# Row-tiled scores in two softmax attentions: queries and keys of four heads stacked together, max and exp passes interleaved, masks grouped, loops unrolled

## Chip, cores and metric

The kernel runs on one NeuronCore of one Trainium2 chip. The metric is the device time of one execution in microseconds, and lower is better. The kernel before was timed three times.

## What is computed

The reference is a two-layer decoder on x of 4 sequences x 256 tokens x 128 channels. Each layer is attention, cross attention and a mixture of experts. The change touches two of the six parts: the first (called at0 in the kernel: rotary self attention) and the fifth (xa1: causal cross attention). Both have 16 heads of 8 channels and a plain softmax over 256 keys:

```python
x = x + _L0_attn_ref(_layernorm(x), wq, wk, wv)             # at0, touched
x = x + _L0_xattn_ref(_layernorm(x), ctx, ctx, ...)         # xa0
x = x + _L0_ffn_ref(_layernorm(x), ...)                     # ff0
x = x + _L1_attn_ref(_layernorm(x), ...)                    # at1
x = x + _L1_xattn_ref(_layernorm(x), ctx, mask, ...)        # xa1, touched
x = x + _L1_ffn_ref(_layernorm(x), ...)                     # ff1
# at0
scores = jnp.einsum('bqhd,bkhd->bhqk', q, k) / jnp.sqrt(HEAD_DIM)
out = jnp.einsum('bhqk,bkhd->bqhd', softmax(scores), xv)
# xa1: the same with a causal mask, then a projection
m = mask[:, None, :, None] + future[None, None, :, :]
scores = jnp.where(m != 0, NEG, scores)
ctx = jnp.einsum('bhqk,bkhd->bqhd', softmax(scores), v).reshape(b, s, d)
return ctx @ WO
```

## The kernel before

One program per engine, tied by semaphores. The kernel goes through the six parts in order. An attention works on one sequence (b, "batch", 256 tokens) at a time, and in it on head after head; `step(k, b, follow)` is one slot of a software pipeline of 32 slots per batch, of which each batch overlaps the second 16 with the first 16 of the next. So 80 slots run per attention, 16 of them filling and 16 of them emptying. What one head passes through:

- **Stacking.** TensorE copies the 8 query rows of four heads (a "group" g; head h = 4g + j) to rows 32j to 32j+23 in PSUM with a selection matrix `selr`, in float32r with a high and a low part (`stack`, L1135 to L1140: one matmul of the high part, one of the low part). Three copies (high, low and high parts for the one operand, the matching ones for the other) keep the accuracy of float32 in one pass. ScalarE moves the result to `qs` (`stacked_queries`, L529) and to `ks` (`stacked_keys`, L483).
- **Key copies.** The score matmul contracts over all 128 rows, so for each head the keys must be zero outside its 32 rows. SyncE copies the 32 rows of head h from `ks` to `km[:, h, :]`, a buffer of zeros, with one DMA per head (`attention_keys`, L286 to L304): 64 DMAs per attention.
- **Max pass** (slot k = h, L1171 to L1190): scores with queries on the partitions, two matmuls of 256 columns (one for each 128 queries) into PSUM bank h % 2; in xa1 each is followed by a bfloat16 matmul that adds the causal mask (L1189). VectorE takes the negative maximum of each query (L788, one instruction per head) into `nmax`.
- **Merge** (slots 5, 9, 13, 17): TensorE transposes the maxima of a group (L1198), and VectorE adds them to `qs` as a 25th row (L795), where `ks` holds ones (bias `one_row`).
- **Exp pass** (slot k = h + 7, L1201 to L1213): scores with keys on the partitions, two matmuls of 256 columns into bank 2 + h % 2, in xa1 again each with a mask matmul (L1212). ScalarE applies exp (L546) into `prob`.
- **Values** (slots 12 + 4g and 13 + 4g, L1227): float32 matmuls with 32 output columns per head, four heads beside each other on the four column tiles of the array, first the keys 0 to 127, in the next slot the keys 128 to 255.
- **Outputs** (slots 27, 28): transposes back to tokens (L1249), division and residual on VectorE (L802 to L819); in xa1 also slots 30, 31 with the projection (L1254, L1259, L823).

Every engine runs its instructions in order. The score banks are two per pass, so the matmuls of head h wait for the reduction (or exp) of head h - 2. `pipelined` (L227) lays the slots out: batch 0 and batch 3 are written out, batches 1 and 2 are a hardware loop (`Fori`). The fill of batch 0 has the stacking of its keys already behind it (`stack_first_keys`) and stacks the first queries ahead of slot 0. In a batch, slots 3, 4, 9, 10 stack queries and slots 7, 8, 15 stack keys of the next one.

## Time and profile before

| what | us |
|---|---|
| three timed executions, median | 581.61 |
| lowest, highest | 576.68, 583.44 |
| profiled execution, span | 581.3 |
| PE busy in it | 504.7 (87%) |
| DVE busy | 442.6 (76%) |
| ACT busy | 250.3 (43%) |
| POOL busy | 121.2 (21%) |

The profiled execution is described by its span of 581.3 us, 0.3 under the median of the timed ones. PE is TensorE's matmuls, PEld its weight loads (they overlap PE), DVE VectorE, ACT ScalarE, POOL GpSimd, SP the DMA queue of SyncE. A matmul is listed with its pipeline latency, so the distance between the starts of two neighbours, not the time listed, is what one costs in a stream. Matmuls of float32r are listed as f32. In this profile at0 spans about 31 to 117 us, xa1 about 238 to 355 us.

### The profile page before, as it was taken

How to read it: one execution, taken by the hardware profiler on the slowest of the kernel's cores; microseconds unless marked ns; L12 is line 12 of the kernel's file. 1: busy time of each engine (PE TensorE's matmuls, PEld its weight loads, DVE VectorE, ACT ScalarE, POOL GpSimd, SP SyncE). 2: the span in 40 equal slices, each digit the busy share in tenths (PEclk: the TensorE clock that was granted, in tenths of full speed). 3: DMA queues.
4: the chain of work that ended last, by engine and by line, in shares of the span. 5: the costliest groups of instructions: out<-in, count | busy, mean ns of one | idle time of the engine just before them, and what ended most of it. 6: DMA issues, size and time to landing. Idle time of an engine off the chain costs nothing.

```text
span 581.3 us, 9298 instructions
## 1 busy us (share of the span) xinstructions
PE 504.7 (87%) x2860; PEld 366.1 (63%) x2860; DVE 442.6 (76%) x939; ACT 250.3 (43%) x488; POOL 121.2 (21%) x147
## 2 busy tenths in 40 slices
PE   2889999789926865799999987999999999999995
PEld 1566776567404542577777765777767676767673
DVE  4396777574696876575656648899999999999996
ACT  1556675422542110334444444464544545362651
POOL 5060001111555251200000000021212111212112
PEclk9989999978976776799999997999999999999998
DMA  8711110003000000101000000000000000000001
GB/s 295 299 38 33 28 27 19 1 1 145 1 1 0 1 1 0 25 21 27 22 18 19 19 1 1 1 1 2 0 0 0 0 0 0 0 0 2 0 1 36
DMA packets 12750, 15.77 MB, mean 27 GB/s; under 512 B 4136, under 2 KB 11432, under 8 KB 12080
## 3 DMA queue, kind: packets, MB, share of 16 engines
q1 hardware_dynamic: 12288, 14.53, 8.0%
q10 hardware_dynamic: 432, 0.85, 0.4%
q8 instruction: 17, 0.28, 0.2%
q14 instruction: 13, 0.11, 0.1%
HBM read 10.65 MB, written 0.52 MB: 19 GB/s over the span
## 4 chain that ended last, share of the span: by engine, by line
PE 53%; DVE 22%; issue 15%; ACT 5%; POOL 2%; DMA 1%; DVEq 1%; ACTq 0%; POOLq 0%
PE ps L1185 7%; PE ps L1227 6%; PE ps L1208 5%; DVE bigr L1034 4%; PE ps L1444 3%; PE ps L1445 2%; PE ps L1446 2%; PE ps L1189 2%; POOL xnT L449 2%; DVE big L1043 2%; PE ps L1383 2%; PE ps L1344 2%; PE ps L1249 1%; PE ps L1212 1%; PE ps L1463 1%
## 5 line engine op out<-in xcount | busy, mean ns | idle before, releaser
L788 DVE TENSOR_REDUCE nmax<-ps 128x2 f32<-128x512 f32 x128 | 86.5, 690 | 47.8 <-PE ps L1189 31.1
L1036 DVE TENSOR_TENSOR bigr<-big,bigr 128x512 fp32r<-128x512 f32 x128 | 111.1, 868 | 4.4
L546 ACT ACTIVATE big<-ps 128x512 f32<-128x512 f32 (+1 forms) x128 | 68.9, 545 | 76.2 <-PE ps L1212 51.1
L657 ACT ACTIVATE big<-ps,b 128x512 f32<-128x512 f32 x128 | 85.3, 694 | 19.3 <-DVE bigr L1036 11.1
L449 POOL TENSOR_TENSOR xnT<-xnT,big 128x512 f32<-128x512 f32 x32 | 44.1, 1377 | 174.5 <-DVE big L1043 174.4
L1185 PE MATMUL ps<-bigr,qs 128*128 128x256 f32 x256 | 69.3, 345 | 4.4 <-DVE nmax L788 2.1
L1208 PE MATMUL ps<-qs,bigr 128*128 128x256 f32 x256 | 65.6, 328 | 1.1 <-ACT big L546 1.1
L1185 PEld LDWEIGHTS ps<-bigr,qs 128*128 128x128 f32 x256 | 45.2, 196 | 25.4 <-DVE nmax L788 14.5
L1444 PE MATMUL ps<-k1hi,w1hi 128*128 128x512 f32 x128 | 55.7, 435 | 0.4
L1034 DVE CAST bigr<-big 128x512 fp32r<-128x512 f32 x128 | 53.6, 419 | 0.9 <-ACT big L657 0.9
L1445 PE MATMUL ps<-k1hi,w1lo 128*128 128x512 f32 x128 | 51.9, 406 | 0.0
L1446 PE MATMUL ps<-k1lo,w1hi 128*128 128x512 f32 x128 | 51.8, 405 | 0.0
L1461 PE MATMUL ps<-bigr,w2hi 128*128 128x512 f32 x128 | 50.8, 397 | 0.2
L1463 PE MATMUL ps<-bigr,w2hi 128*128 128x512 f32 x128 | 50.5, 395 | 0.0
L1462 PE MATMUL ps<-bigr,w2lo 128*128 128x512 f32 x128 | 50.2, 392 | 0.0
L1208 PEld LDWEIGHTS ps<-qs,bigr 128*128 128x128 f32 x256 | 44.8, 194 | 3.6 <-ACT big L546 2.2
L1227 PE MATMUL ps<-big,vaug 128*32 128x256 f32 (+1 forms) x512 | 37.3, 364 | 1.4 <-ACT big L546 1.4
L347 POOL COPY vaug<-v_tok 128x64 f32 x32 | 7.3, 240 | 135.4 <-PE ps L1227 135.4
L1444 PEld LDWEIGHTS ps<-k1hi,w1hi 128*128 128x128 f32 x128 | 24.9, 195 | 12.9 <-issue 6.1
L650 ACT ACTIVATE big<-ps 128x512 f32<-128x512 f32 x32 | 19.2, 600 | 26.5 <-PE ps L1452 26.4
L1189 PE MATMUL ps<-trib,identb 128*128 128x256 bf16 (+1 forms) x128 | 30.4, 256 | 0.0
L1212 PE MATMUL ps<-trib,identb 128*128 128x128 bf16 x128 | 29.4, 230 | 0.0
(192 smaller groups left out, 886.9 us busy)
## 6 DMA issues: line engine op xcount, KB each, us to landing
bigr<-ks SPq DMA_DIRECT2D x128, 32.0 KB, 1.9
wi<-in_wi SPq DMA_DIRECT2D x1, 2048.0 KB, 7.8
wo<-in_wo SPq DMA_DIRECT2D x1, 2048.0 KB, 12.2
big<-in_sel SPq DMA_DIRECT2D x1, 1024.0 KB, 8.8
wo<-in_w SPq DMA_DIRECT2D x1, 1024.0 KB, 4.8
wi<-in_w SPq DMA_DIRECT2D x1, 1024.0 KB, 8.2
x<-in_x SPq DMA_DIRECT2D x1, 512.0 KB, 5.0
ctxT<-in_ctxT ACTq DMA_DIRECT2D x1, 512.0 KB, 6.6
```

The lines of the kernel that those rows point to most:

```text
L546: act.activation(prob[:, h % 8, c], ps[:, 2 + h % 2, c], ACT.Exp, scale=DH ** -0.5).then_inc(s(L + "_exp"), 1)
L657: act.activation(gel[:, c, :], ps[:, c, :], ACT.Gelu_apprx_tanh, bias=b1[:, u % E1, c:c + 1]).then_inc(s("ff1_gel"), 1)
L788: v.tensor_reduce(nmax[:, :, g, col:col + 1], ps[:, k % 2, :].rearrange("p (t k) -> p t k", t=TPB), AX.X, ALU.max, negate=True).then_inc(s ...
L1034: v.tensor_copy(ghi[:, u % 2, c, :], gel[:, c, :]).then_inc(s("ff1_ghi"), 1)
L1036: v.tensor_tensor(glo[:, u % 2, c, :], gel[:, c, :], ghi[:, u % 2, c, :].bitcast(f32), ALU.subtract).then_inc(s("ff1_glo"), 1)
L1185: last = pe.matmul(ps[:, h % 2, at:at + T], qs[:, h // HPG, t * P:t * P + P], km[:, h, :], start=True, stop=not causal)
L1208: last = pe.matmul(ps[:, 2 + h % 2, at:at + T], km[:, h, t * P:t * P + P], qs[:, h // HPG, :], start=True, stop=not causal)
L1227: last = pe.matmul(ps[QUAD * j:QUAD * j + QUAD, 4, (g % 2) * T + first:(g % 2) * T + T], vaug[:, t, h, :], prob[:, h % 8, place(t) * T + f ...
L1444: pe.matmul(ps[:, k, :], w1hi[:, e, f], xhi[:, c], start=True, stop=False)
L1445: pe.matmul(ps[:, k, :], w1lo[:, e, f], xhi[:, c], start=False, stop=False)
L1446: pe.matmul(ps[:, k, :], w1hi[:, e, f], xlo[:, c], start=False, stop=True).then_inc(s("ff1_up"), 1)
L1463: last = pe.matmul(o, w2hi[:, e, k, :], glo[:, u % 2, k, :], start=False, stop=(k == FC - 1))
```

## The change

Queries and keys of a group are stacked into one buffer `qk` [128, group, side, 256] by four matmuls that contract over the 32 rows of the group's channels only, in one PSUM bank; one ScalarE instruction moves both. A score matmul of head h takes the 32 rows 32j to 32j+31 of `qk` for both operands, so the zero-filled `km`, its fill and its 128 DMAs are gone. In each slot the two max matmuls of head k and the two exp matmuls of head k - 7, which lie on neighbouring 32-row tiles of the array, alternate. In xa1 the mask matmuls of both passes follow the four score matmuls, and the second exp matmul has only the 128 query columns that the mask leaves. The value matmuls of a group stand together in one slot (k % 4 = 0). All four stacks of batch 0 come ahead of slot 0; later stacks come in slots 13, 15, 3 and 9. The 80 slots are written out, with no loop.

```diff
+FIRST_BANKS = (6, 7, 4, 5)
...
-        qs = sb("qs", [P, G, T], f32r)
-        ks = sb("ks", [P, G, T], f32r)
-        km = bigr[:, 4096:8192].rearrange("p (h t) -> p h t", h=H)
+        qk = sb("qk", [P, G, 2, T], f32r)
...
+        AFT_SLOT = 2
+        STACK_SLOTS = {13: (1, 0), 15: (1, 1), 3: (0, 2), 9: (0, 3)}
+        STACKED_SLOTS = {14: (1, 0), 0: (0, 1), 4: (0, 2), 10: (0, 3)}
...
+        def pipelined(slot, beside={}):
+
+            for b in range(B + 1):
                 for k in range(H):
-                    if not first:
-                        step(H + k, b - 1, follow)
-                    step(k, b, follow)
-
-            for k in range(H // 2 - 1, H):
-                step(k, -1, True)
-            if before_first:
-                before_first()
-            batch(0, True, True)
-            if before_loop:
-                before_loop()
-            with engine.Fori(1, B - 1) as b:
-                batch(b, False, True)
-            batch(B - 1, False, False)
-            for k in range(H, 2 * H):
-                step(k, B - 1, None)
-                if k in beside:
-                    beside[k]()
+                    slot(k, b)
+                    if b == B and k in beside:
+                        beside[k]()
...
-            def attention_keys(L):
-
-                def keys(b, g):
-                    if g % 2 == 0:
-
-                        sp.wait_ge(s(L + "_ksev"), 1 + 2 * b + g // 2 + 1)
-                        sp.sem_inc(s("keys_stacked"), 1)
-
-                    sp.wait_ge(s(L + "_s"), H * b + HPG * g + HPG)
-                    for j in range(HPG):
-                        rows = slice(QUAD * j, QUAD * j + QUAD)
-                        sp.dma_start(km[rows, HPG * g + j, :].bitcast(f32), ks[rows, g, :].bitcast(f32)
-                                     ).then_inc(s(L + "_km%d" % g), 16)
-
-                for g in range(G):
...
-            pool.memset(km[:, :, :].bitcast(f32), 0.0).then_inc(s("const"), 1)
...
+            def evacuate_stack(L, b, g, bank=6):
+
+                act.wait_ge(s(L + "_stk"), G * b + g + 1)
+                act.activation(qk[:, g, :, :], ps[:, bank, :].rearrange("p (a t) -> p a t", a=2),
+                               ACT.Identity, bias=one_row[:, :]).then_inc(s(L + "_stkev"), 1)
...
+                    if stack := stacked(STACKED_SLOTS, k, b):
+                        evacuate_stack(L, *stack)
+                    if b == B and not causal and k == AFT_SLOT + 1:
                         evacuate_aft_sums(0)
-                    if 7 <= k < H + 7:
-                        h = k - 7
-                        if there(b):
-                            act.wait_ge(s(L + "_s"), H + H * b + h + 1)
-
-                            if h % HPG == 0:
-                                act.wait_ge(s(L + "_pv"), G + G * b + h // HPG - 1)
-
-                            c = slice(P if causal else 0, TPB * T)
-                            act.activation(prob[:, h % 8, c], ps[:, 2 + h % 2, c], ACT.Exp, scale=DH ** -0.5
-                                           ).then_inc(s(L + "_exp"), 1)
-
-                    if k in (5, 7) and there(b):
-                        stacked_queries(b, 2 + k // 7)
-                    if k in (12, 15) and follow:
-                        stacked_queries(b + 1, k // 15)
-                    if k in (8, 15) and follow and there(b):
-                        stacked_keys(L, b + 1, int(k == 15))
-                    if k in (17, 25) and there(b):
-
-                        gg = k // 8 - 2
-                        act.wait_ge(s(L + "_pv"), G + G * b + 2 * gg + 2)
+                    if head := lagging(k, b, 7):
...
+                def stack(b, g, bank=6):
+
+                    if g == 0 and b * T % HALF == 0:
+                        pe.wait_ge(*half_ready[b * T // HALF])
+                    if b > 0:
+                        pe.wait_ge(s(L + "_stkev"), G * b + g)
+                    rows, c = slice(QUAD * g, QUAD * g + QUAD), slice(b * T, b * T + T)
+                    for side, (hi, lo) in enumerate(sides):
+                        o = ps[:, bank, side * T:side * T + T]
+                        pe.matmul(o, selr[rows, side, g, 0, :], hi[rows, c], start=True, stop=False)
+                        last = pe.matmul(o, selr[rows, side, g, 1, :], lo[rows, c], start=False, stop=True)
+                    last.then_inc(s(L + "_stk"), 1)
+
+                def head_rows(h):
+                    j = h % HPG
+                    return slice(QUAD * j, QUAD * j + QUAD)
+
+                def max_scores(b, h):
+                    if h % HPG == 0:
+                        pe.wait_ge(s(L + "_stkev"), G * b + h // HPG + 1)
+                    pe.wait_ge(s(L + "_red"), H * b + h + 1)
+                    rows, g = head_rows(h), h // HPG
+                    for t in range(TPB):
+                        at = place(t) * T
+                        yield pe.matmul(ps[:, h % 2, at:at + T], qk[rows, g, 0, t * P:t * P + P], qk[rows, g, 1, :],
+                                        start=(t == 0 or not causal), stop=not causal)
+
+                def exp_scores(b, h):
+                    if h % HPG == 0:
+                        pe.wait_ge(s(L + "_mrg"), 1 + G * b + h // HPG + 1)
+                    pe.wait_ge(s(L + "_exp"), H * b + h + 1)
+                    rows, g = head_rows(h), h // HPG
+                    for t in range(TPB):
+                        at, first = place(t) * T, P if causal and t else 0
+                        yield pe.matmul(ps[:, 2 + h % 2, at + first:at + T], qk[rows, g, 1, t * P:t * P + P],
+                                        qk[rows, g, 0, first:T], start=(t == 0 or not causal), stop=not causal)
+
+                def max_masks(h):
+                    for t in range(TPB):
+                        at = place(t) * T
+                        last = pe.matmul(ps[:, h % 2, at + t * P:at + T], identb[:, :], trib[:, 0:TPB - t, :],
+                                         start=False, stop=(t == TPB - 1))
+                    return last
+
+                def exp_masks(h):
+                    for t in range(TPB):
+                        at = place(t) * T
+                        last = pe.matmul(ps[:, 2 + h % 2, at + t * P:at + t * P + P], identb[:, :],
+                                         trib[:, TPB, :], start=False, stop=(t == TPB - 1))
+                    return last
+
+                def scores(k, b):
+
+                    new = max_scores(b, k) if b < B else iter(())
+                    head = lagging(k, b, 7)
+                    old = exp_scores(*head) if head else iter(())
+                    last_new = last_old = None
+                    for t in range(TPB):
+                        last_new, last_old = next(new, None), next(old, None)
+                    if causal and b < B:
+                        last_new = max_masks(k)
+                    if causal and head:
+                        last_old = exp_masks(head[1])
+                    if b < B:
+                        last_new.then_inc(s(L + "_mx"), 1)
+                    if head:
+                        last_old.then_inc(s(L + "_s"), 1)
...
+                def values(b, g):
+                    pe.wait_ge(s(L + "_vaug"), G * b + g + 1)
...
+                def slot(k, b):
+                    if aft_sums and b == B and k == AFT_SLOT:
+                        pe.wait_ge(s(L + "_red"), 2 + H * B)
+                        aft_sums(0)
+                    scores(k, b)
+                    if next_stack := stacked(STACK_SLOTS, k, b):
+                        stack(*next_stack)
+                    if k % HPG == 1 and (group := lagging(k, b, 5)):
+                        transposed_maxima(group[0], group[1] // HPG)
+                    if k % HPG == 0 and (group := lagging(k, b, 12)):
+                        values(group[0], group[1] // HPG)
+                    if k in (11, 12) and b >= 1:
+                        token_rows(b - 1, k - 11)
+                    if causal and k in (14, 15) and b >= 1:
+                        projected(b - 1, k)
+
+                for g in range(G):
+                    stack(0, g, FIRST_BANKS[g])
+                pipelined(slot, beside)
...
-            stack_first_keys("xa1", k1hi[:, :], k1lo[:, :])
...
+            pe.wait_ge(s("xa1_lo"), 2)
+            attention("xa1", True, k1hi[:, :], k1lo[:, :], ((s("xa1_lo"), 1), (s("xa1_lo"), 2)),
+                      beside={8: lambda: transpose_xn("ff1", 0, 1), 11: first_logits})
```

Two places show the new order on TensorE. The first is at0 with all passes running. Before (L1227 values, L1185 max pass, L1198 transposed maxima, L1208 exp pass; register instructions are the loop's counters):

```order
L1227 MATMUL ps<-big,vaug 32x256 x4
L1182 REGISTER_ALU
L1185 MATMUL ps<-bigr,qs 128x256 x2
L1196 REGISTER_ALU
L1198 MATMUL ps<-ident,nmax 128x128 x2
L1205 REGISTER_ALU
L1208 MATMUL ps<-qs,bigr 128x256 x2
L1182 REGISTER_ALU
L1185 MATMUL ps<-bigr,qs 128x256 x2
```

and of the change (L1177 values, L1115 max pass, L1125 exp pass, L1165 transposed maxima):

```order
L1177 MATMUL ps<-big,vaug 32x256 x8
L1115 MATMUL ps<-qk 128x256
L1125 MATMUL ps<-qk 128x256
L1115 MATMUL ps<-qk 128x256
L1125 MATMUL ps<-qk 128x256
L1165 MATMUL ps<-ident,nmax 128x128 x2
L1115 MATMUL ps<-qk 128x256
L1125 MATMUL ps<-qk 128x256
L1115 MATMUL ps<-qk 128x256
L1125 MATMUL ps<-qk 128x256
```

The values of both key halves stand together, max and exp matmuls alternate, and the transposes of the maxima stand alone between matmuls on 32-row tiles.

The second is xa1, a slot with transposed maxima and the next one, before (L1189 mask of the max pass, L1212 mask of the exp pass):

```order
L1185 MATMUL ps<-bigr,qs 128x256
L1189 MATMUL ps<-trib,identb 128x256
L1185 MATMUL ps<-bigr,qs 128x256
L1189 MATMUL ps<-trib,identb 128x128
L1198 MATMUL ps<-ident,nmax 128x128 x2
L1208 MATMUL ps<-qs,bigr 128x256
L1212 MATMUL ps<-trib,identb 128x128
L1208 MATMUL ps<-qs,bigr 128x256
L1212 MATMUL ps<-trib,identb 128x128
```

and of the change, up to the second score group (L1131 and L1138 masks):

```order
L1115 MATMUL ps<-qk 128x256
L1125 MATMUL ps<-qk 128x256
L1115 MATMUL ps<-qk 128x256
L1125 MATMUL ps<-qk 128x128
L1131 MATMUL ps<-trib,identb 128x256
L1131 MATMUL ps<-trib,identb 128x128
L1138 MATMUL ps<-trib,identb 128x128 x2
L1165 MATMUL ps<-ident,nmax 128x128 x2
L1115 MATMUL ps<-qk 128x256
L1125 MATMUL ps<-qk 128x256
```

Each slot now goes once from 32-row tiles to the whole array and back.

## Rows read from the trace of the kernel before

**Rows 1.** The page: the whole program, busy time and share of the span.

```profile
span 581.3 us, 9298 instructions
PE 504.7 (87%) x2860; PEld 366.1 (63%) x2860; DVE 442.6 (76%) x939; ACT 250.3 (43%) x488; POOL 121.2 (21%) x147
bigr<-ks SPq DMA_DIRECT2D x128, 32.0 KB, 1.9
```

**Rows 2.** Stretches: a batch of at0, one of xa1, 15 steps of xa1's last.

```profile
core 0: us, PE busy (x) PEld busy (x) DVE busy (x) ACT busy (x) POOL busy (x), PEclk, DMA share, GB/s
66.25:85.02 18.77, 18.31 (x163) 13.31 (x161) 13.24 (x26) 12.65 (x25) 0.95 (x4) 1.00 0.13 30
...
290.95:316.54 25.59, 24.82 (x233) 19.11 (x231) 14.85 (x29) 11.42 (x25) 0.95 (x4) 1.00 0.09 21
...
316.54:338.20 21.66, 21.11 (x200) 16.21 (x199) 14.20 (x29) 8.79 (x19) 0.71 (x3) 1.00 0.05 13
```

**Rows 3.** Groups by shape in 66.25 to 85.02, one batch of at0.

```profile
L788 DVE TENSOR_REDUCE nmax<-ps 128x2 f32<-128x512 f32 x16 | 10.7, 688 | 4.9 <-PE ps L1185 4.9
L1227 PE MATMUL ps<-big,vaug 128*32 128x256 f32 x64 | 5.1, 391 | 0.0
...
L531 ACT ACTIVATE qs<-ps 128x256 fp32r<-128x256 f32 x4 | 1.5, 379 | 0.0
...
L488 ACT ACTIVATE ks<-ps,one_row 128x512 fp32r<-128x512 f32 x2 | 1.4, 688 | 0.0
```

**Rows 4.** Timeline of at0, a run of matmuls of 256 columns: start, us, engine.

```profile
64.22 0.19 PEld L1137 LDWEIGHTS ps<-bigr,selr 128*128 128x128 f32 x1
...
64.57 0.19 PEld L1138 LDWEIGHTS ps<-bigr,selr 128*128 128x128 f32 x1
```

**Rows 5.** Timeline of at0, values between score matmuls.

```profile
66.05 0.38 PE L1198 MATMUL ps<-ident,nmax 128*128 128x128 f32 x2
...
66.16 0.30 PEld L1208 LDWEIGHTS ps<-qs,bigr 128*128 128x128 f32 x2
...
66.60 0.64 PE L1227 MATMUL ps<-big,vaug 128*32 128x256 f32 x8
...
67.17 0.30 PEld L1185 LDWEIGHTS ps<-bigr,qs 128*128 128x128 f32 x2 [0.41 <-DVE nmax L788]
```

**Rows 6.** Timeline of xa1, values of 128 columns.

```profile
291.50 0.16 PEld L1227 LDWEIGHTS ps<-big,vaug 128*32 128x32 f32 x8
...
291.86 0.19 PEld L1185 LDWEIGHTS ps<-bigr,qs 128*128 128x128 f32 x1 [0.20 <-DVE nmax L788]
```

**Rows 7.** Timeline of xa1, score and mask matmuls in turn.

```profile
292.34 0.20 PEld L1208 LDWEIGHTS ps<-qs,bigr 128*128 128x128 f32 x1
...
293.07 0.20 PEld L1185 LDWEIGHTS ps<-bigr,qs 128*128 128x128 f32 x1
```

**Rows 8.** Timeline at the start of at0.

```profile
30.45 0.68 DVE L735 TENSOR_TENSOR big<-ps,rope 128x512 f32<-128x512 f32 x1
...
32.92 0.42 DVE L763 TENSOR_TENSOR big<-big 128x256 f32<-128x256 f32 x1
33.26 1.28 DVE L788 TENSOR_REDUCE nmax<-ps 128x2 f32<-128x512 f32 x2
...
34.00 0.38 PE L1185 MATMUL ps<-bigr,qs 128*128 128x256 f32 x1 [1.80 <-DVE nmax L788]
```

**Rows 9.** Stretch after it, with TensorE's granted clock (PEclk).

```profile
34.50:37.80 3.30, 3.20 (x15) 3.06 (x14) 2.78 (x6) 1.84 (x3) 3.30 (x4) 0.50 0.21 50
```

**Rows 10.** Timeline at the start of xa1.

```profile
245.62 0.69 DVE L997 TENSOR_TENSOR bigr<-ps,bigr 128x512 fp32r<-128x512 f32 x1 [1.54 <-ACT bigr L644]
246.37 0.19 PEld L1185 LDWEIGHTS ps<-bigr,qs 128*128 128x128 f32 x1 [1.15 <-DVE bigr L997]
```

**Rows 11.** Timeline of GpSimd at the program's start.

```profile
2.76 3.52 POOL L329 MEMSET bigr<- 128x4096 f32 x1
...
7.26 0.23 POOL L338 TENSOR_SCALAR vare<-mv 128x4 f32<-128x4 f32 x1 [0.78 <-DVE mv L713]
```

262 lines of the change are left out of this document (89 added, 173 removed).

## Prediction

> **What bounds the kernel now.** I read the page first: TensorE is busy for 504.7 of 581.3 us, VectorE for 442.6, and the 128 key copies of SyncE land in 1.9 us each [rows 1]. That is an average over six stages, so the second view is the table of stretches, one full batch of each attention [rows 2]. The reader should see TensorE busy for 18.3 of 18.8 us in at0 and for 24.8 of 25.6 us in xa1, with VectorE at 13.2 and 14.9. TensorE bounds both, by little in at0 and by much in xa1. No score matmul waits for a key copy there, so removing the DMAs frees nothing by itself. The groups by shape [rows 3] show VectorE's 16 reductions of 0.69 us and only 4.9 us of waiting in front of them: this is all the room that a faster TensorE has in at0.
>
> The third view is the timeline, read for distances between starts. In a stream of 256-column matmuls one costs 0.12 us (64.22 to 64.57 for three) [rows 4]. Value matmuls on column tiles cost more around them than in them. The last two score weight loads start at 66.16, so the next would come at 66.40; the values' loads come at 66.60 and the score stream resumes at 67.17 with a weight load that nothing hides (0.12 more) [rows 5]. Half a group of values thus takes 0.77 us. With 128 columns in place of 256 the stretch from 66.60 to 67.17 is 0.36 (291.50 to 291.86) instead of 0.57 us [rows 6], so the columns themselves are 0.42 of the 0.77 and 0.34 us is the price of switching the array to column tiles and back. The eight instructions have a mean of 0.39 us each and are through in 0.64 together [rows 3, 5]: neighbouring tiles do work at the same time, their weight loads too. In xa1 a score matmul with its mask costs 0.245 us (292.34 to 293.07 for three) [rows 7].
>
> **The rule beside it.** The Trainium skill, "TensorEngine Tiling (Array Packing)", section "Key Properties", says that a change of the tiling mode drains the engine. The trace agrees for column tiles, with the 0.34 us above; no row here has 32-row tiles. By that rule the change pays for its overlap with drains: with no drain, the terms of 0.34 below would go, and the result would be near 545; with them it is the forecast.
>
> **At0, a full batch.** Before: 64 score matmuls x 0.12 = 7.7, 16 stack matmuls x 0.12 = 1.9, 16 transposes x 0.11 (66.05 to 66.16 [rows 5]) = 1.8, 8 halves of values x 0.77 = 6.2; sum 17.6, measured 18.8, so 1.2 us of waiting. After: if max and exp matmuls run side by side, 32 steps x 0.12 = 3.8. Stacks 1.9 and transposes 1.8 stay (a stack's four matmuls share one row tile and cannot overlap). Values in one block a group: 4 x (0.85 + 0.34) = 4.8. New: transposes of maxima (4) and outputs (2) now stand between 32-row matmuls, 6 x 0.34 = 2.0. Sum 14.3. But now VectorE is at 13.2, and it can be only two banks behind. Its own step is 0.6 to 0.69 us (two reductions in 1.28 [rows 8]). A group of four slots has one slot of 0.24 + 1.19 = 1.43 (values), one of 0.24 + 0.56 = 0.8, or 1.3 with a stack, and two in which VectorE's step of about 0.65 us rules: 3.8 to 4.0, times four 15.6, plus 1.5 for the outputs: 17.1; with a little of the old waiting 17.6. So 1.2 us a batch of the 3.3 that TensorE gains. The bounds: nothing, if all of it is lost in waiting (18.8), and 14.5 if VectorE alone ruled.
>
> Two full batches give 2.4, the first and last together 0.6 (fill and tail have only one of the two passes, so nothing overlaps), and the merged values of the tail 0.5. At the start all four stacks (16 matmuls, 1.9 us) now stand ahead of slot 0 behind the last rotation, which ends at 31.13. The first reduction started at 33.26, behind VectorE's own maximum at 32.92 [rows 8], so the stacks show only by 0.3 us. In exchange TensorE no longer stands idle for the 1.80 us before 34.00 [rows 8]. That pause was followed by 3.3 us at half clock [rows 9], some 1.2 GHz instead of 2.4; I count 0.6 back. At0: 2.4 + 0.6 + 0.5 + 0.3 = 3.8 us.
>
> **Xa1, a full batch.** Before: 64 x 0.245 = 15.7, stacks 1.9, 18 transposes and 4 projections x 0.11 = 2.4, values 4 x (0.77 + 0.55) = 5.3; 25.3, measured 25.6. After, a slot is: two steps side by side, 0.24; masks of 256 + 3 x 128 = 640 columns at 0.107 per 256, with starts 0.31; one switch to 32-row tiles and back. For the switch I take the nearest row, 0.34 [rows 5]. That is 0.89 for a slot that cost 0.98, and 16 x 0.89 = 14.2. Stacks 1.9, with two extra switches where transposes follow a stack 0.7; transposes and projections 2.4; values 4 x (0.64 + 0.2), since half their switch belongs to the next slot already, 3.4. Sum 22.6; with the waiting of before and some for the two banks 23.8: 1.8 us a batch. No row shows a switch to 32-row tiles, so its price is bounded from both sides: below by 0.2, the gap on entering alone (66.40 to 66.60 [rows 5]), which would give 16 x 0.14 = 2.2 us more per batch; above by 0.55, that gap on top of the 0.34, which would give 3.4 us less, slower than before.
>
> Two full batches give 3.6, the last 1.2, the tail 0.3, the first nothing: its seven filling slots have no overlap and now pay the switch, but the reduction's pace hides it. The start pays. Today's first max matmul follows the last low part of the queries at once (246.31 to 246.37 [rows 10]), as keys and half the queries are stacked before. Now 16 matmuls come in between, 13 to 16 x 0.12 = 1.6 us, with nothing above them. Xa1: 3.6 + 1.2 + 0.3 - 1.6 = 3.5 us.
>
> **Edits at nothing.** SyncE's copies and their semaphores: no one waited. GpSimd's fill of `km` ends at 6.28, and GpSimd then still waits 0.78 us for VectorE's statistics [rows 11]; with no cover it would be 3.5. ScalarE's moves: four of about 0.69 per batch in place of 2 x 0.69 and 4 x 0.38 [rows 3], 2.8 against 2.9 us, in a batch of which ScalarE works 12.65 of 18.77 us; with no cover, one of 0.69 would show at the start. The loop: xa1's written-out last batch takes 21.66 us for 15 steps of 16 [rows 2]; a mean sixteenth (1.44) and the 12 stack matmuls it lacks (1.4) make 24.5 against the loop's 25.6. So unrolling gives up to 1.1 us a batch; I take nothing, since the missing step holds values and is longer than the mean. Whichever of these is late, the next in line is VectorE in at0 and still TensorE in xa1.
>
> **Sum.** 581.3 - 3.8 - 3.5 = 574.0 us. The profiled span is 0.3 us under the median of the timed runs, which changes nothing at this size.
>
> **Rivals.**
> (A) *The row tiles do not overlap* (the change doesn't do what it says). For it: the trace shows overlap of column tiles only, and a float32r weight load of 128 columns is hardly hidden behind a 256-column matmul at 0.12. If loads of different row tiles go one after the other, at0 gets 14.3 + 3.8 = 18.1 us of TensorE's work a batch and with the 1.2 of waiting 19.3, 0.5 more than before, four times 2; a slot of xa1 grows by 0.19 (two more steps, one of 128 columns), so a batch to 23.8 + 3.0 = 26.8, 1.2 more than before, four times 5; its filling slots 1, its start 1.9: 581.3 + 2 + 5 + 1 + 1.9 = 591. The Trainium skill, "TensorE: Matmul & The Clock Gate", section "LDWEIGHTS (loading the stationary operand)", says that a 32x128 load takes as long as a 128x128 one. No run here shows it yet; it would make this case, unless the loads overlap too.
> (B) *Dear switches*: side by side, but entering and leaving 32-row tiles costs 0.55 us or more. With 16 switches a batch in xa1 and 6 in at0, 88 in all, the forecast's 7.3 us are gone at 0.08 us more, so it decides from 0.42 us on. At 0.55, xa1 loses 3.4 x 4 = 14 of the forecast and at0 1.3 x 4 = 5, of which half hides behind VectorE: about 590.
> (C) *Cheap switches*, 0.2 us: xa1 gains 2.2 x 4 = 9 more, at0 2 more: 563.
> (D) *The gain drowns in lockstep*: at0 gives nothing and xa1 half: 581.3 - 1.8 = 579.5. For it: 4.9 us of waiting in front of the reductions is spread in gaps of 0.4.
>
> **How the numbers follow.** Forecast 0.45 (its own range 568 to 579), (C) 0.15, (D) 0.14, (A) 0.14, (B) 0.12. A measurement of this kernel tells about 1% from no change, 5.8 us, so faster means under 575.8. Of the forecast's 0.45 some two thirds lie there, with (C) 0.45; slower is (A) and (B), 0.26; the rest, 0.29, is the same. The range for 8 in 10 cuts the ends of (C) and of (A) and (B): 561 to 593.
>
> **What would show it.** Right: in the new trace, max and exp matmuls of a slot start a few ns apart in pairs, with 0.12 us between pairs; at0's full batch (16 reductions) takes 17.6 us, xa1's 23.8; a switch to 32-row tiles and back costs 0.3 to 0.4; the first reduction of xa1 comes 1.6 us later after VectorE's low part. Wrong: score matmuls 0.12 apart one by one (A), gaps over 0.25 on each side of the masks (B) or under 0.1 (C), reductions of at0 at 18.8 per 16 with TensorE idle (D).

## Result and profile after

| | us |
|---|---|
| changed kernel, median of 4 (lowest, highest) | 598.36 (591.72, 601.23) |
| kernel before beside it, median of 4 | 581.04 |
| ratio, 95% interval | 1.026 [1.019, 1.034] |
| profiled execution after, span | 597.6 |

The change makes the kernel 2.6% slower; 574.0 was forecast, and 598.4 lies above the range of 561 to 593. (Medians are taken over all executions of a kernel; the ratios, here and below, leave out those whose time lies over 1.5% above its fastest.) The page of the changed kernel, busy times and granted clock in 40 slices of 14.9 us:

```profile
PE 521.2 (87%) x2860; PEld 355.8 (60%) x2860; DVE 443.9 (74%) x939; ACT 250.3 (42%) x472; POOL 117.4 (20%) x146
...
PEclk9865675688995797655599998899999999999998
```

and the clock row of the kernel before, slices of 14.5 us:

```profile
PEclk9989999978976776799999997999999999999998
```

VectorE, ScalarE and GpSimd do what they did [rows 1]. TensorE executes as many matmuls and is busy 16.5 us longer. The clock row tells where: slices 3 to 8 are at0, 18 to 20 the filling and first batch of xa1, and there the digits are 5 to 7 where the row of before has an 8 and 9s. The same by batches. Each stretch below runs from the first reduction of a batch to the first of the next: four of at0, the last with 15 steps, then three of xa1.

```profile
core 0: us, PE busy (x) PEld busy (x) DVE busy (x) ACT busy (x) POOL busy (x), PEclk, DMA share, GB/s
33.40:49.70 16.30, 14.74 (x84) 10.25 (x88) 11.53 (x20) 10.04 (x17) 6.88 (x10) 0.51 0.01 2
49.70:73.80 24.10, 23.81 (x165) 14.34 (x168) 13.67 (x26) 12.18 (x23) 0.94 (x4) 0.55 0.00 1
73.80:94.70 20.90, 20.71 (x164) 12.85 (x167) 13.52 (x26) 12.69 (x23) 0.95 (x4) 0.69 0.01 2
94.70:117.90 23.20, 22.65 (x151) 13.30 (x150) 12.84 (x25) 10.93 (x20) 3.04 (x4) 0.55 0.00 1
264.20:289.40 25.20, 25.20 (x134) 15.78 (x134) 12.23 (x20) 6.21 (x12) 0.24 (x1) 0.50 0.01 2
289.40:315.40 26.00, 26.00 (x233) 17.12 (x231) 15.08 (x30) 11.69 (x23) 0.94 (x4) 0.79 0.00 1
315.40:336.80 21.40, 21.40 (x232) 14.78 (x230) 15.05 (x29) 11.62 (x23) 0.94 (x4) 1.00 0.01 2
```

The kernel before had 14.3, 18.7, 18.8 and 16.0 us for the four of at0, with the clock at 1.00 but for some 3 us at the start, and 18.2, 25.6 and 25.6 for the three of xa1. The third and the last of these are in [rows 2]; the first of each attention are

```profile
33.30:47.54 14.24, 13.44 (x99) 11.10 (x99) 11.52 (x21) 9.27 (x18) 6.93 (x10) 0.88 0.14 32
...
247.10:265.30 18.20, 17.89 (x153) 14.12 (x152) 11.70 (x19) 7.17 (x16) 0.24 (x1) 1.00 0.10 24
```

Only the last stretch of the table is wholly at full clock, and it takes 4.2 us less than before, not more. The time is lost where the clock is 0.50 to 0.79. From its first reduction to its 64th, at0 takes 84.5 us (33.4 to 117.9) where it took 67.7 (33.3 to 101.0). Xa1 takes 91.4 (264.2 to 355.6) where it took 91.1: what the last batches gain, the first ones lose. So at0 accounts for 16.8 us, which is all of the 16.3 between the two profiled executions; the rest of the program comes to -0.5 in sum.

**What the change does at either clock.** Timeline of TensorE in at0 at half clock, a slot of scores and the transposed maxima behind it (start, length, engine, line, operation):

```profile
51.51 0.58 PE L1115 MATMUL ps<-qk 32*128 32x256 f32 x1
51.52 0.58 PE L1125 MATMUL ps<-qk 32*128 32x256 f32 x1
51.89 0.41 PE L1115 MATMUL ps<-qk 32*128 32x256 f32 x1
51.89 0.41 PE L1125 MATMUL ps<-qk 32*128 32x256 f32 x1
52.23 0.69 PE L1165 MATMUL ps<-ident,nmax 128*128 128x128 f32 x2
```

and at full clock, a slot with values behind it:

```profile
77.03 0.35 PE L1115 MATMUL ps<-qk 32*128 32x256 f32 x1
77.03 0.38 PE L1125 MATMUL ps<-qk 32*128 32x256 f32 x1
77.22 0.27 PE L1115 MATMUL ps<-qk 32*128 32x256 f32 x1
77.26 0.28 PE L1125 MATMUL ps<-qk 32*128 32x256 f32 x1
77.46 1.07 PE L1177 MATMUL ps<-big,vaug 128*32 128x256 f32 x16
```

Max and exp matmuls start within 0.04 us of each other: the row tiles do overlap, at both clocks. (In one slot of a group they don't start together: the exp matmuls wait for VectorE's merge of the maxima, 0.33 us at 79.74 to 80.07.) The four score matmuls take 0.43 us to the values (77.03 to 77.46) against 0.72 to the transposes at half clock (51.51 to 52.23). A whole group of four slots of at0 takes 3.73 us at full clock (77.03 to 80.76, from the scores of one value slot to those of the next) and 5.60 at half (49.72 to 55.32, from one reduction of VectorE to the fourth after it). The first two groups of a full batch took 4.23 and 4.40 before.

Timeline of xa1 at full clock, a plain slot and the start of the next:

```profile
318.03 0.38 PE L1115 MATMUL ps<-qk 32*128 32x256 f32 x1
318.07 0.38 PE L1125 MATMUL ps<-qk 32*128 32x256 f32 x1
318.25 0.27 PE L1115 MATMUL ps<-qk 32*128 32x256 f32 x1
318.29 0.22 PE L1125 MATMUL ps<-qk 32*128 32x128 f32 x1
318.46 0.34 PE L1131 MATMUL ps<-trib,identb 128*128 128x256 bf16 x2
...
318.84 0.38 PE L1100 MATMUL ps<-bigr,selr 32*128 32x256 f32 x1
```

The slot takes 0.81 us (318.03 to 318.84); 0.89 was forecast, and it was 0.98 before.

### The profile page after: what moved, and what is told of

Same layout as the page of the kernel before. It is cut to its first block, busy times and chain, and to the rows that moved or that the text cites. A ratio compares the mean times of both kernels' runs of the same rounds, so it can differ in the third digit from the quotient of the medians.

```text
span 597.6 us, 8661 instructions
## 1 busy us (share of the span) xinstructions
PE 521.2 (87%) x2860; PEld 355.8 (60%) x2860; DVE 443.9 (74%) x939; ACT 250.3 (42%) x472; POOL 117.4 (20%) x146
## 4 chain that ended last, share of the span: by engine, by line
PE 60%; DVE 20%; issue 12%; ACT 4%; POOL 2%; DMA 1%; DVEq 1%; ACTq 0%; POOLq 0%
PE ps L1115 10%; PE ps L1177 7%; PE ps L1131 4%; PE ps L1399 3%; PE ps L1400 3%; PE ps L1401 3%; DVE bigr L985 2%; PE ps L1165 2%; PE ps L1418 2%; PE ps L1189 2%; PE ps L1417 2%; PE ps L1416 2%; POOL xnT L419 2%; PE ps L1125 2%; PE ps L1100 2%
## 5 line engine op out<-in xcount | busy, mean ns | idle before, releaser
L606 ACT ACTIVATE big<-ps,b 128x512 f32<-128x512 f32 x128 | 85.2, 694 | 18.7 <-DVE bigr L987 10.6
L1115 PE MATMUL ps<-qk 32*128 32x256 f32 x256 | 79.7, 413 | 4.1 <-DVE nmax L736 2.7
L1125 PE MATMUL ps<-qk 32*128 32x256 f32 (+1 forms) x256 | 73.0, 386 | 0.7 <-ACT big L503 0.7
L1115 PEld LDWEIGHTS ps<-qk 32*128 32x128 f32 x256 | 51.1, 252 | 33.0 <-issue 20.1
L1125 PEld LDWEIGHTS ps<-qk 32*128 32x128 f32 x256 | 48.9, 239 | 4.2 <-ACT big L503 2.6
L1177 PE MATMUL ps<-big,vaug 128*32 128x256 f32 (+1 forms) x512 | 42.0, 459 | 1.4 <-ACT big L503 1.4
L1401 PEld LDWEIGHTS ps<-k1lo,w1hi 128*128 128x128 f32 x128 | 25.0, 195 | 6.1
L1416 PEld LDWEIGHTS ps<-bigr,w2hi 128*128 128x128 f32 x128 | 24.1, 188 | 6.3 <-DVE bigr L987 1.0
```

The source lines that it names most:

```text
L606: act.activation(gel[:, c, :], ps[:, c, :], ACT.Gelu_apprx_tanh, bias=b1[:, u % E1, c:c + 1]).then_inc(s("ff1_gel"), 1)
L1115: yield pe.matmul(ps[:, h % 2, at:at + T], qk[rows, g, 0, t * P:t * P + P], qk[rows, g, 1, :], start=(t == 0 or not causal), stop=not causal)
L1125: yield pe.matmul(ps[:, 2 + h % 2, at + first:at + T], qk[rows, g, 1, t * P:t * P + P], qk[rows, g, 0, first:T], start=(t == 0 or not caus ...
L1177: last = pe.matmul(ps[QUAD * j:QUAD * j + QUAD, 4, (g % 2) * T + first:(g % 2) * T + T], vaug[:, t, h, :], prob[:, h % 8, place(t) * T + f ...
L1401: pe.matmul(ps[:, k, :], w1hi[:, e, f], xlo[:, c], start=False, stop=True).then_inc(s("ff1_up"), 1)
L1416: pe.matmul(o, w2hi[:, e, k, :], ghi[:, u % 2, k, :], start=(k == 0), stop=False)
```

## Experiments

The question: why does the clock fall, and what do the parts of the change bring without it? The theories were that short gaps between small matmuls let the clock fall (more work in the gaps would hold it); that the changes of tiling mode do it; and that it is the few rows of the array in which a 32-row matmul works.

One table for all that follows: the time at half clock between the first and the last (64th) reduction of each attention, in us, added up from the granted clock of stretches of 0.5 us in each run's trace. At0 starts with a drop in every run, the kernel before too; what differs is how long it lasts and whether there are others.

| run | rows of a score matmul | at0 | xa1 |
|---|---|---|---|
| before | 128 | 3 | 0 |
| e11: masks grouped, values merged | 128 | 3 | 0 |
| e3 | 128 | 7 | 4 |
| e10: e3 with a 32-row matmul a slot | 128 | 17 | 15 |
| e9 | 72 | 51 | 29 |
| e7 | 64 | 41 | 79 |
| changed kernel | 32, two tiles side by side | 72 | 36 |
| e2 | 32, one tile | 82 | 107 |

**e1: filler work.** Two 512-column matmuls over the whole array ahead of the transposed maxima of each group.

```diff
                     pe.wait_ge(s(L + "_mrg"), G * b + g + 1)
+                    for _ in range(2):
+                        pe.matmul(ps[:, 5, :], selr[:, 0, 0, 0, :], selr[:, 0, 0:2, :, :], start=True, stop=True)
```

> The changed kernel with two more matmuls of 512 columns on the whole array ahead of the transposed maxima of each group (their result is overwritten). In the changed kernel a group of four slots of at0 takes 5.60 us in the stretches at half clock and 3.73 at full clock, and xa1's batches took 26.0 and 21.4. Theory W (the clock falls because 32-row tiles leave the array mostly unused): more whole-array work holds full clock in most of both attentions, so in spite of 32 x 0.43 = 14 us more of work the kernel gets faster than the change, 575 to 590, mean clock over 0.9. Theory G (the clock falls because TensorE pauses for VectorE): the pauses shrink too, so it also recovers in at0, but xa1's first half, in which TensorE was busy throughout, stays as it is. Theory S (dear mode switches, clock beside the point): time rises by 14 us or more, to 610.

Measured: 598.79 us, 1.030 [1.021, 1.039]. The second and third batch of at0:

```profile
50.30:77.00 26.70, 26.36 (x172) 16.02 (x176) 13.88 (x27) 12.17 (x23) 0.95 (x4) 0.57 0.00 1
77.00:94.80 17.80, 17.42 (x172) 11.10 (x176) 13.83 (x27) 12.36 (x23) 0.95 (x4) 1.00 0.01 2
```

A miss: the time is that of the changed kernel, though a granted clock of 1.00 returned and stayed for the rest of at0, which it did not do there. The filler starts ahead of the first transposed maxima (34.75 us), when the clock has been at half for over 2 us already. It does not bring the clock back soon (it is at half up to 73 us in at0), and e7 below holds 1.00 over the second half of at0 without any filler, so e1 doesn't show that the filler held it. The second line is worth something by itself: with the filler in it, the batch at full clock takes 17.8 us against 18.8 before.

**e2: no overlap, rows as in the change.** The exp matmuls go to the row tile of the max matmuls beside them (the diff is of the exp pass; the exponentials are those of permuted heads).

```diff
-                    rows, g = head_rows(h), h // HPG
+                    rows, g = head_rows(h + 7), h // HPG
```

> The exp pass takes the rows of another head of its group, those that lie on the row tile of the max pass of the same slot: it computes the exponentials of permuted heads, with every instruction's size as it was, and nothing can overlap between the two passes. Theory W: TensorE's instructions take longer, its pauses get shorter, but each matmul still uses 32 rows; the clock stays low (mean at most 0.85) and the time rises over the change by the lost overlap, 0.24 us a slot at full and 0.45 at half clock, 80 + 80 slots less the 14 fill and tail slots each: 620 to 640. Theory G: busier, so full clock holds, 590 to 600.

Measured: 651.75 us, 1.123 [1.113, 1.133], beyond the 620 to 640 of theory W and far from the 590 to 600 of G. A batch of at0, one of xa1, and a slot at full clock:

```profile
48.80:75.80 27.00, 26.71 (x162) 17.29 (x162) 13.92 (x27) 11.96 (x23) 0.95 (x4) 0.56 0.00 1
304.30:341.80 37.50, 37.50 (x232) 26.70 (x230) 15.40 (x29) 12.06 (x24) 0.95 (x4) 0.58 0.00 0
```

```profile
103.66 0.38 PE L1115 MATMUL ps<-qk 32*128 32x256 f32 x1
...
104.33 0.44 PE L1165 MATMUL ps<-ident,nmax 128*128 128x128 f32 x2
```

On one tile the four take 0.67 us (103.66 to 104.33) instead of 0.43: the overlap is worth 0.24 a slot, which is the forecast's two times 0.12. TensorE is busy for 99% of the batch, and the clock is 0.56 all the same. Gaps are not what keeps it low: fuller with 32-row matmuls, it falls more often. The changed kernel shows it too. Its clock fell a second time in at0 at 81.6 us, with no pause of TensorE above 0.19 us from 78 us on, and stayed at half in a stretch without any:

```profile
82.00:94.70 12.70, 12.70 (x84) 8.15 (x79) 7.00 (x15) 6.16 (x11) 0.47 (x2) 0.50 0.00 1
```

("Busy" holds the pipeline latency of each matmul, so pauses shorter than that don't show in it.)

**e3: all 128 rows.** Both passes contract over all rows (so the scores are sums over four heads); no overlap, and no change of tiling mode for scores. Both passes get the same edit, here and in e7 and e9.

```diff
-                    rows, g = head_rows(h), h // HPG
+                    rows, g = slice(0, P), h // HPG
```

> Both passes contract over all 128 rows of the stacked buffers, so each score is the sum over the four heads of a group (wrong numbers, the same instructions in the same order and with the same waits). Order, grouped masks, stacks and the written-out slots are those of the change; only the row tiles, their overlap and the switches for them are gone. Theory W: full clock nearly throughout as before the change (mean 0.92 or more), at0's batch near 18 us, xa1's near 25: 575 to 585. Theory S: the same, since the switches are gone. Theory G: at0 pauses as little as before, full clock too. So this run prices what the rest of the change is worth without row tiles: I expect 0 to -5 us against before.

Measured: 567.6 us, 0.977 [0.970, 0.984], better than the 575 to 585 expected. A full batch of at0 and of xa1:

```profile
46.90:65.90 19.00, 18.93 (x162) 13.91 (x160) 13.62 (x26) 12.92 (x23) 0.95 (x4) 1.00 0.00 1
...
267.60:289.20 21.60, 21.60 (x233) 18.35 (x232) 14.87 (x30) 11.69 (x23) 0.94 (x4) 1.00 0.00 1
```

The clock stays at 1.00 in the batches; it is at half for 7 us at the start of at0 and for 4 at that of xa1. With the same number of matmuls, order and copies as in the changed kernel, it is 31 us faster. Rows and switches changed together here, so the next three runs part them.

**e7: 64 rows.** Two tiles of 64 rows in place of four of 32.

```diff
-                    rows, g = head_rows(h), h // HPG
+                    half, g = h % HPG // 2, h // HPG
+                    rows = slice(64 * half, 64 * half + 64)
```

> The changed kernel with score matmuls that contract over 64 rows, the half that holds the head's tile: each score is the sum over two heads (wrong numbers, same instructions and waits). The two passes of a slot lie on different halves in half of the slots and overlap there. Theory W (the clock depends on how many rows the matmuls work): between the change (mean clock 0.84) and full rows (0.92), so 0.87 to 0.90, and 575 to 590. If 64 rows suffice: clock 0.92 and about 563, less than full rows, because of the overlap. If rows are not it, but overlap is: 0.85, 590 to 595.

Measured: 619.02 us, 1.066 [1.059, 1.074]. Two batches of at0 and one of xa1:

```profile
50.40:78.00 27.60, 27.36 (x165) 17.55 (x164) 13.94 (x27) 12.66 (x22) 0.95 (x4) 0.58 0.00 1
78.00:96.40 18.40, 18.21 (x161) 12.41 (x160) 13.35 (x26) 12.64 (x23) 0.95 (x4) 1.00 0.00 1
290.80:331.20 40.40, 40.40 (x232) 27.53 (x230) 15.39 (x30) 11.89 (x23) 0.94 (x4) 0.50 0.00 0
```

The size was missed (575 to 590 or 590 to 595 expected): 64 rows are no half-way house. The clock was at half for 109 us in one piece, the first 30 of them ahead of xa1's first reduction and 79 in its scores. It also stayed at 1.00 over the second half of at0, where the changed kernel's fell again. So the same matmuls run for long at half clock and, once it has returned, can hold it. The changed kernel shows this as well: the last two stretches of xa1, on 32-row tiles like the first, are at 1.00 throughout.

**e9: 72 rows, no mode switch.** Every score matmul contracts over the first 72 rows, which is no row tile (only the stacks, as in e3, work on 32-row tiles).

```diff
-                    rows, g = head_rows(h), h // HPG
+                    rows, g = slice(0, 72), h // HPG
```

> The changed kernel with score matmuls that contract over the first 72 rows (sums over heads, wrong numbers; instructions and waits the same). With more than 64 rows they are no tile of their own, so the array is not switched for them, as in the full-row run (567.6 us, clock 0.92); in rows they stand next to the 64-row run (619.0 us, clock 0.83). Theory R (rows decide the clock): like the 64-row run, clock under 0.87, over 600 us. Theory D (the drains of the mode switches, two a slot, leave the array empty often enough to lose the clock): like full rows, clock 0.92, 568 us.

Measured: 598.73 us, 1.030 [1.025, 1.036], with a mean clock of 0.85 to 0.88 in its executions (e3: 0.92 to 0.93): theory R but for its "over 600". Two batches of at0 and the third of xa1:

```profile
53.30:82.50 29.20, 29.20 (x161) 21.48 (x160) 14.11 (x27) 13.18 (x22) 0.95 (x4) 0.56 0.00 1
82.50:102.80 20.30, 20.23 (x161) 14.65 (x160) 13.58 (x26) 12.85 (x23) 0.95 (x4) 0.92 0.01 2
...
313.20:334.80 21.60, 21.60 (x232) 18.37 (x230) 14.86 (x29) 11.73 (x23) 0.95 (x4) 1.00 0.01 2
```

At full clock the xa1 batch takes the 21.6 us of e3, so no switch is paid. The same program as e3 but for 56 rows, and the clock is at half for 44 us in one piece in at0 and for 41 around the start of xa1 (29 of them behind its first reduction). It needs no score matmul on a row tile and no switch for that.

**e10: 128 rows, with the switches.** As e3, with a matmul of 32 rows and 32 columns ahead of each max pass, so that every slot enters a row tile and leaves it.

```diff
+                    pe.matmul(ps[:, h % 2, 0:32], qk[0:QUAD, g, 0, 0:P], qk[0:QUAD, g, 1, 0:32], start=True, stop=True)
```

> The full-row run with one more matmul of 32 rows and 32 columns ahead of each max pass (its result is overwritten): each slot goes to a 32-row tile and back, as in the change, while all score matmuls use 128 rows. Theory R: clock as with full rows, 0.90 or more, and 128 x 0.3 us of switches on top where TensorE bounds: 567.6 + 25 to 38 = 593 to 606. Theory D: clock falls to 0.85 or less, with stretches of 30 us and more at half clock in the attentions, over 615 us.

Measured: 609.25 us, 1.049 [1.045, 1.053], 3 us above the 593 to 606 of theory R and below the 615 of D. A batch of at0 and of xa1:

```profile
54.00:76.50 22.50, 22.50 (x177) 16.49 (x177) 14.01 (x27) 13.13 (x23) 0.95 (x4) 1.00 0.01 1
288.00:314.50 26.50, 26.50 (x249) 21.36 (x246) 15.13 (x29) 11.73 (x23) 0.94 (x4) 1.00 0.00 1
```

The clock stands at 1.00 in both full batches although every slot switches twice. At the start of each attention it is different: the half clock lasts for 17 us in at0 and 15 in xa1, where e3 has 7 and 4; the miss of 3 us can lie there. Whether the switches or the few rows of the added matmul prolong it isn't told apart. So the pair e9 and e10 decides the main question, with a rest: few rows hold the clock down without switches (51 and 29 us); switches with 128 rows do not in the batches, and at most, with the added matmul, lengthen the half clock at the start of each attention by some 10 us. It prices the switch too: (22.5 - 19.0) / 16 = 0.22 us a slot in at0, (26.5 - 21.6) / 16 = 0.31 in xa1, both ways and the small matmul together.

**e4: only xa1 changed.** At0 as in the kernel before, with its loop and key copies; the diff is against that kernel, cut to where the two meet (xa1's new code on each engine is that of the change).

```diff
-        qs = sb("qs", [P, G, T], f32r)
-        ks = sb("ks", [P, G, T], f32r)
+        qk = sb("qk", [P, G, 2, T], f32r)
+        qs, ks = qk[:, :, 0, :], qk[:, :, 1, :]
...
-            attention_keys("xa1")
```

> at0 is that of the kernel before, xa1 that of the change. at0 then costs what it did (31 to 117 us). Theory W: xa1 as in the change, its first half at half clock: 598 less the loss in at0, which by the two traces is 12 us or more of it, 581 to 588. If the half clock of xa1's start depends on what went before it, it may be at full clock at once: 568. Theory S: xa1 loses as much as at0, 590.

Measured: 582.38 us, 1.000 [0.995, 1.005]. The first two batches of xa1:

```profile
251.30:276.40 25.10, 25.10 (x134) 15.76 (x134) 12.17 (x19) 6.16 (x12) 0.24 (x1) 0.50 0.00 1
276.40:299.20 22.80, 22.80 (x233) 15.37 (x230) 15.07 (x29) 11.63 (x23) 0.94 (x4) 0.93 0.01 1
```

The whole loss goes when at0 keeps its old code; in xa1 the start and the filling slots at half clock give back what the later batches gain (the third takes 21.4 us). The 581 to 588 of theory W holds it.

**e8: full-array work ahead of xa1.** e4 with eight whole-array matmuls of 256 columns where the early key stacks stood.

```diff
+            for _ in range(8):
+                pe.matmul(ps[:, 7, 0:T], selr[:, 0, 0, 0, :], selr[:, 0, 0, :, :], start=True, stop=True)
             pe.wait_ge(s("ld_xa1"), 64)
```

> at0 as before, xa1 as in the change, with eight matmuls of 256 columns on the whole array in the place where the key stacks of the kernel before stood, ahead of xa1's projections (their result is not used). Without them TensorE was at half clock from 221 to 279 us, and the first reduction of xa1 came at 251.3 instead of 247.1. Theory W: the projections run at full clock and the first reduction comes at 248 to 249, but the filling slots (max pass on 32-row tiles alone) let the clock fall again within the first batch, so 3 to 6 us less than without: 577 to 579. If what matters is only that TensorE was at full clock on entering: both xa1 batches at 21.4 and full clock, 568.

Measured: 588.07 us, 1.013 [1.007, 1.019]. The first two batches:

```profile
243.60:268.80 25.20, 25.20 (x134) 15.76 (x134) 12.23 (x20) 6.18 (x12) 0.24 (x1) 0.50 0.01 2
268.80:301.30 32.50, 32.50 (x232) 20.56 (x230) 15.22 (x29) 11.80 (x23) 0.94 (x4) 0.60 0.00 1
```

The first reduction comes 7.7 us earlier than in e4 (243.6 against 251.3; how much of that is due to the eight matmuls is open, since the parts ahead of xa1 differ by a few us between executions). The projections, which ran at half clock in e4, run at 1.00 from 233.4 us on. But at 240.4 us, with the stacks and behind a wait of 1.41 us for VectorE, the clock falls, 3 us ahead of the first reduction, and it stays at half for 55 us. So 577 to 579 was missed, xa1's scores did not begin at full clock, and what they would do from there wasn't tested.

**e5, e6 and e11: the parts that need no row tile**, on the kernel before. e5 groups the masks per pass in xa1 and gives the second exp matmul 128 columns:

```diff
-                                             start=True, stop=not causal)
-                            if causal:
-
+                                             start=(t == 0 or not causal), stop=not causal)
+                        if causal:
+                            for t in range(TPB):
+                                at = place(t) * T
                                 last = pe.matmul(ps[:, h % 2, at + t * P:at + T], identb[:, :], trib[:, 0:TPB - t, :],
-                                                 start=False, stop=True)
+                                                 start=False, stop=(t == TPB - 1))
...
-                            at = place(t) * T
-                            last = pe.matmul(ps[:, 2 + h % 2, at:at + T], km[:, h, t * P:t * P + P], qs[:, h // HPG, :],
-                                             start=True, stop=not causal)
+                            at, first = place(t) * T, P if causal and t else 0
+                            last = pe.matmul(ps[:, 2 + h % 2, at + first:at + T], km[:, h, t * P:t * P + P],
+                                             qs[:, h // HPG, first:T], start=(t == 0 or not causal), stop=not causal)
```

> The kernel before with one part of the change: in xa1 the two mask matmuls of a pass follow its two score matmuls, and the second exp matmul has 128 columns. All score matmuls keep 128 rows and their key copies. Theory M (the float32r weight load is not hidden behind the bfloat16 mask matmul before it, so each alternation costs about 0.12 us): two alternations a slot go, 16 x 0.25 = 4 us less in a batch of 25.6, half of it if only one per pass goes: 12 to 16 us in all, 565 to 570. Theory V (the full-row run owed its 13 us to the merged values and the written-out slots): under 3 us, 578 to 581. Clock as before the change.

Measured: 570.81 us, 0.985 [0.981, 0.989], just above theory M's 565 to 570 (half of the 4 us a batch that it priced came). e6 is e5 with the values of a group in one block in xa1, e11 has the block in at0 too (the diff is e6's; in e11 `merged` is `range(TPB)` and the condition `k % HPG < 1`, for both attentions):

```diff
-                    if 12 <= k < 28 and k % HPG < TPB and now:
-
-
-                        g, t = (k - 12) // HPG, k % HPG
+                    merged = range(TPB) if causal else (k % HPG,)
+                    for t in (merged if 12 <= k < 28 and k % HPG < (1 if causal else TPB) and now else ()):
+
+
+                        g = (k - 12) // HPG
```

> The same, and in xa1 the value matmuls of both key halves of a group stand in one slot. One switch to column tiles and back goes per group, 0.34 x 16 = 5.4 us of TensorE's work; TensorE bounds xa1, so by theory M 3 to 5 us under the run with masks alone (about 563). If the longer block makes VectorE wait instead, no difference.

Measured: 566.66 us, 0.976 [0.970, 0.981], 4 us under e5.

> The kernel before with the masks grouped per pass and the values of a group in one block in xa1, and now the block in at0 too (each head still contracts over 128 rows with its key copy). Price theory: a switch to column tiles and back costs 0.34 us, at0 has eight of them a batch, and the block leaves four. Then four times 0.34 = 1.4 us a batch would go, but in the first and last batch and beside VectorE (13.2 us of 18.8 busy) part of it is hidden: a full batch of at0 17.8 to 18.4 instead of 18.8, the whole 1 to 3 us under the version with the block in xa1 alone (566.7), so 563.5 to 565.5. Rival: the block holds the next pair of scores back by 0.7 to 0.8 us at a stretch, the two banks are too few to cover it, and VectorE waits for it: at0's batch 18.8 to 19.5 and the time 567 to 570. Either way the granted clock stays at 1.00 in the batches, as all scores work on 128 rows; a half-clock stretch in at0 beyond the first 4 us would speak against the theory of rows.

Measured: 564.67 us, 0.970 [0.966, 0.974], the fastest version. A full batch of xa1 in e5, then in e6:

```profile
262.00:285.50 23.50, 22.58 (x234) 18.19 (x231) 14.79 (x29) 11.42 (x25) 0.95 (x4) 1.00 0.11 25
```

```profile
262.40:284.80 22.40, 21.48 (x233) 18.48 (x231) 14.80 (x29) 11.07 (x25) 0.95 (x4) 1.00 0.11 26
```

and a full batch of at0 in e11:

```profile
66.60:84.80 18.20, 17.77 (x164) 13.75 (x161) 13.18 (x26) 12.03 (x24) 0.95 (x5) 1.00 0.13 30
```

The masks' part takes 2.1 us off each full batch of xa1 (25.6 to 23.5), merging the values another 1.1, and in at0 0.6 (18.8 to 18.2). From the first to the 64th reduction at0 goes from 67.9 us in e6 to 65.9 in e11.

e5 changes two things, and its timeline tells them apart in part. A max pass and the exp pass behind it:

```profile
292.83 0.48 PE L1185 MATMUL ps<-bigr,qs 128*128 128x256 f32 x2
...
293.31 0.43 PE L1209 MATMUL ps<-qs,bigr 128*128 128x256 f32 x2
...
293.67 0.37 PE L1137 MATMUL ps<-k1hi,selr 128*128 x1
```

Either pass took 0.49 us before. The max pass, which is only regrouped, takes 0.48 (292.83 to 293.31): regrouping saves it almost nothing. The exp pass takes 0.36 (293.31 to 293.67); it also lost 128 columns, worth some 0.06 us at the 0.12 of 256 columns [rows 4]. So of the 2.1 us about 1.0 is the narrower matmul (an estimate, 16 times 0.06) and about 1.1 the regrouping, most of it in the exp pass.

The clock is 1.00 in all of these stretches, with the same 128-row matmuls against copies that are zero in 96 rows: what goes with the clock is the rows that an instruction works on, not whether they hold zeros. Beside e6 the interval of e11 overlaps, so the 2 us between them rest on the batches more than on the medians.

## Why the prediction was wrong

The steps, in its order:

- **"The row tiles do not overlap"**, rival (A): false. Where neither waits, pairs start within 0.04 us, their weight loads too, and e2 shows what (A) would cost.
- **The pair's price in at0**, "32 steps x 0.12 = 3.8": too low. The four matmuls of a slot take 0.43 us, 0.19 to 0.22 from the first pair to the second (in e2, too, the first matmul of a slot takes 0.23 and the next 0.11) and 0.20 to what follows on the whole array. But the serial four cost 0.67 as well, so the difference, 0.24 a slot, was right.
- **The group of at0**, 3.8 to 4.0 us (its own terms add up to 3.5 without a stack and 4.0 with one): 3.73 at full clock. A batch would be four of these and 1.5 for the outputs, 16.4 (an estimate; no batch of at0 ran wholly at full clock; e1's of 17.8 less its filler, 4 x 0.43, gives 16.1). Forecast 17.6.
- **The batch of xa1**, 23.8: measured 21.4 at full clock. The slot was mis-sized by 0.08 (0.89 for 0.81), 1.3 us a batch; the rest is waiting that I added and that isn't there (TensorE is busy for 21.40 of 21.40 us).
- **The switch**, 0.34 from bounds of 0.2 to 0.55: e10 gives 0.22 to 0.31. So (B) is false and the truth lies between the forecast and (C).
- **What row tiles bring in xa1.** A full-clock batch gains 4.2 us (25.6 to 21.4). e5 and e6 have 2.1 of them from masks and narrower matmul and 1.1 from values, without row tiles. e3, with all of the change but the scores' row tiles, has 21.6: 0.8 more come with what else e3 has and e6 hasn't (the other stacks, the slots written out, no key copies; not told apart), and 0.2 are left for overlap less switches. The prediction priced the new slot as a whole and never asked what its parts would give by themselves: in xa1 nearly all of the gain needs no row tile. In at0 it is the other way round, 19.0 in e3 against the 16.4 of the estimate.
- **The start of at0**, "the stacks show only by 0.3 us": the first reduction is at 33.4 against 33.26 [rows 8]. Right. But "I count 0.6 back" for the half-clock stretch [rows 9] was the sign that was read the wrong way: I laid it to the pause of 1.80 us ahead of it. That pause became three, of 0.91, 0.70 and 0.85 us (2.46 in sum, with 0.71 + 1.80 = 2.51 before), and the stretch grew from 3 to 38 us; with the same code and 128 rows (e3) it was 7. What starts it may well be the pauses; how long it lasts is set by the work behind them.
- **The start of xa1**, 1.6 us more after VectorE's second low part. From that part to the first reduction it was 1.49 us (245.62 to 247.11 [rows 10]) and is 4.00 now, VectorE and TensorE of the changed kernel:

```profile
260.20 0.69 DVE L948 TENSOR_TENSOR bigr<-ps,bigr 128x512 fp32r<-128x512 f32 x1 [2.85 <-ACT bigr L592]
264.20 0.69 DVE L736 TENSOR_REDUCE nmax<-ps 128x2 f32<-128x512 f32 x1 [3.31 <-PE ps L1131]
```

```profile
260.95 0.62 PE L1100 MATMUL ps<-bigr,selr 32*128 32x256 f32 x4 [1.41 <-DVE bigr L948]
...
262.94 0.79 PE L1115 MATMUL ps<-qk 32*128 32x256 f32 x2 [0.73 <-ACT qk L454]
```

  The 16 stack matmuls run four abreast, so they cost less than their number says, but at half clock, and ScalarE's move stands behind them (0.73 of waiting): 2.5 us more instead of 1.6.
- **"Edits at nothing".** The early key stacks looked free to move. They were 128-row work while TensorE would else have waited; e8 puts such work back, and the clock still falls 7 us later, ahead of the scores, and stays low. So the missing work alone is not the cause, only part of the start's price.

**The step that failed** is none of these: it is the unspoken one that every price read at a granted clock of 1.00 [rows 2] would hold after the change. All four rivals kept it as well. At half clock a group of at0 costs 5.60 us instead of 3.73, and at0 spends 72 of its 84.5 us there. Taken at full clock (estimate: e11's 65.9 us of at0 less 1.8 for each of three batches; xa1 with e6's first batch of 16.7, then twice 21.4 and 18.8), at0 would be some 24 us shorter and xa1 13, so the time about 561. That this is close to rival (C)'s 563 is partly luck: (C) has its gain from cheap switches, and in xa1 most of it is masks, values and written-out slots. The mechanism of overlap was right, its size too small in at0 and, less the switches, close to nothing in xa1; the clock took some 37 us where the change without it gives some 20.

That the clock is low because matmuls work on few rows is shown by e3, e9 and e10: same program, 128 rows hold it in the batches, 72 don't, and 128 rows with switches do. At the start of each attention e10 leaves open what part of the longer half clock is due to switches. That idle time is not what keeps it low is shown by e2 and by the stretch of the changed kernel from 82 to 94.7 us; the first fall of at0 stands behind pauses in every run. What stays open: how the granted clock comes back and why one execution of 32, 64 or 72 rows holds it in one half of an attention and not in the other; and whether some full-row work inside the filling slots themselves, not ahead of them (e8) or behind them (e1), or four row tiles side by side in place of two, would hold it and bring the 561. That wasn't tried.

## What to carry to other kernels

Before a full-array matmul is split into row tiles, ask what the granted clock rests on: the array's rows at work are part of it, a busy TensorE is not enough, and a clock at half costs more than two overlapping tiles give (1.87 us a group of at0 against 0.96). Price the parts of a change that need no row tile by themselves: here grouped masks with one narrower matmul, and merged values, gave 3% at a steady clock. When a profile shows even a short half-clock stretch in a phase that the change makes thinner, give "the clock falls" a chance and a price among the rivals, from the rows of that stretch.
